# Local attention: the second half of the transposed softmax weights is copied by VectorE, at the head of its step

## The reference, cut to what matters

```
def _L0_attn_ref(x, w_attn, w_proj):
    NUM_HEADS = 16
    WINDOW = 64
    ...
    att = jnp.einsum('bnihd,bnjhd->bnhij', q, k) * scale
    att = jax.nn.softmax(att, axis=-1)
    y = jnp.einsum('bnhij,bnjhd->bnihd', att, v)
    y = y.reshape(B, T, C)
    return jnp.einsum('btc,oc->bto', y, w_proj)
...
    x = x + _layernorm(_L0_attn_ref(_layernorm(x, axis=-1), L0_attn_w_attn, L0_attn_w_proj), axis=-1)
```

## Time and profile before

| | |
|---|---|
| median of 3 runs | 1538.36 us (1538.18 to 1543.03) |
| the profiled execution | 1537.03 us |
| its span, first to last instruction | 1535.2 us |
| mean granted TensorE clock | 0.982 |
| busy over the span: PE, DVE, ACT, POOL | 93%, 55%, 47%, 39% |

### The profile page before, as it was taken

One profiled execution on the slowest core, in us unless ns is written; L12 is line 12 of the kernel. 1 busy time (PEld: TensorE's weight loads), 2 busy tenths in 40 slices (PEclk: granted clock), 3 DMA queues, 4 the chain that ended last, 5 costly groups with the idle time before them and its releaser, 6 DMA issues. The chain is left out here.

```text
span 1535.2 us, 36218 instructions
## 1 busy us (share of the span) xinstructions
PE 1425.0 (93%) x13257; PEld 1244.6 (81%) x13257; DVE 849.5 (55%) x1947; ACT 729.0 (47%) x1688; POOL 605.1 (39%) x1133
## 2 busy tenths in 40 slices
PE   5999999899799999999999997998999999999985
PEld 4777777688799999999999996866777777777865
DVE  3666666456233333333343331365778887888762
ACT  3666666431344444444444542243555555555542
POOL 2555555405122212221222111444566776675442
PEclk9999999999899999999999999999999999999998
DMA  5233333254111111111111112521111112111000
GB/s 194 89 109 112 98 104 94 70 158 138 35 35 43 49 42 42 42 49 42 42 42 42 48 41 64 170 66 47 39 60 46 49 57 62 45 53 43 9 15 22
DMA packets 88045, 100.11 MB, mean 65 GB/s; under 512 B 12384, under 2 KB 74720, under 8 KB 87872
## 3 DMA queue, kind: packets, MB, share of 16 engines
q1 hardware_dynamic: 77824, 75.53, 15.7%
q0 software_dynamic: 6480, 17.70, 4.1%
q10 hardware_dynamic: 3568, 4.55, 0.9%
HBM read 63.28 MB, written 34.47 MB: 64 GB/s over the span
## 5 line engine op out<-in xcount | busy, mean ns | idle before, releaser
L891 PEld LDWEIGHTS ex_hb<-ex_xT,lane_w 128*128 128x128 f32 x3124 | 362.4, 193 | 6.5 <-issue 2.8
L891 PE MATMUL ex_hb<-ex_xT,lane_w 128*128 128x128 f32 x3124 | 363.0, 276 | 2.4 <-ACT lane_w L887 2.4
L994 DVE TENSOR_TENSOR ex_gT<-ex_gT,ex_hb 128x384 f32<-128x384 f32 (+1 forms) x142 | 69.3, 488 | 334.4 <-ACT ex_gT L957 307.1
L865 POOL COPY slot_idx<-source 128x1 int32<-128x1 int32 x69 | 37.6, 544 | 413.0 <-PE ex_xb L918 413.0
L927 PE MATMUL ex_yb<-w,ex_gT 128*128 x852 | 195.7, 379 | 1.6 <-DVE ex_gT L996 1.6
L955 ACT ACTIVATE ex_gT<-ex_hb 128x384 f32<-128x384 f32 (+1 forms) x142 | 62.2, 438 | 246.7 <-PE ex_hb L891 245.9
L927 PEld LDWEIGHTS ex_yb<-w,ex_gT 128*128 128x128 f32 x852 | 156.3, 190 | 20.1 <-issue 1.8
L887 ACT COPY lane_w<-w 128x1408 f32 x71 | 96.9, 1365 | 7.9 <-issue 1.7
L1068 POOL TENSOR_SCALAR la_ln_ve<-la_ln_mv 128x1 f32<-128x1 f32 x128 | 33.4, 261 | 155.6 <-DVE la_ln_mv L1061 150.6
L1639 POOL DMA_INDIRECT la_a<-yg,place x64 | 69.2, 1081 | 49.8 <-POOLq L55 34.6
L1398 DVE TENSOR_TENSOR la_em<-la_E,consts 128x512 f32<-128x512 f32 x128 | 79.3, 681 | 6.6 <-PE la_E L1352 6.5
(11 more groups left out here) (263 smaller groups left out, 3124.7 us busy)
## 6 DMA issues: line engine op xcount, KB each, us to landing
yg<-ex_yo SPq DMA_DIRECT2D x71, 128.0 KB
w<-in_w SPq DMA_DIRECT2D x16, 384.0 KB, 4.8
w<-in_w SPq DMA_DIRECT2D x16, 352.0 KB
w<-in_w SPq DMA_DIRECT2D x16, 320.0 KB
wa_xa<-in_x SPq DMA_DIRECT2D x32, 128.0 KB, 2.1
x<-wa_xo SPq DMA_DIRECT2D x32, 128.0 KB
xn<-wa_xn SPq DMA_DIRECT2D x32, 128.0 KB, 3.5
xn1T<-wa_x1T SPq DMA_DIRECT2D x32, 128.0 KB, 3.5
```

What stands on the lines that cost most here:

```text
L891: o = e.matmul(out, lane_w[:, i % 2, k, at:at + P], B[i % 2]["xT"][:, k, :], start=(k == 0), stop=(k == KC - 1))
L994: o = e.tensor_tensor(g, g, chunks(hb[2 * half + 1][:, 0:n], c1 - c0), ALU.mult)
```

## The change

ScalarE no longer copies the second half. VectorE does it, as the first work of the step behind (step s - 4 = i where ScalarE had it at s - 3 = i), with the same waits ahead of it and the same semaphore after it. ScalarE keeps the first half, at its old place. No other line differs.

```
             for s in range(STEPS):
+                for i in tile(s, 4, NT):
+                    e.wait_ge(S["pTp"], i + 1)
+                    if i >= 2:
+                        e.wait_ge(S["pv"], i - 1)
+                    e.tensor_copy(B[i % 2]["pT"][:, 4:8, :], chunks(bP[:, 1], 4)).then_inc(S["pTb"], 1)
                 for i in tile(s, 3, NT):
                     d = B[i % 2]
                     e.wait_ge(S["S"], i + 1)
...
                     if i >= 2:
                         e.wait_ge(S["pv"], i - 1)
                     e.copy(B[i % 2]["pT"][:, 0:4, :], chunks(bP[:, 0], 4)).then_inc(S["pTa"], 1)
-                    e.copy(B[i % 2]["pT"][:, 4:8, :], chunks(bP[:, 1], 4)).then_inc(S["pTb"], 1)
```

## The result

The changed kernel takes 1524.8 us, the median of 4 runs (1521.97 to 1526.08), beside 1538.27 us for the kernel before (1536.88 to 1543.03, 4 runs). The ratio is 0.9899, with a 95% interval of 0.9877 to 0.9922: it is 1.0% faster. Forecast were 1523.5 us and a range of 1518.5 to 1530. The profiled execution took 1526.08 us, its span is 1524.2 (before: 1535.2), the mean granted clock 0.978 (before: 0.982).

The account below looks back on a forecast made before the run. TensorE was taken to bound the kernel, standing still ahead of L410 for the `pT` copies. 31 steps x 0.48 us = 14.9 us, so 1538.4 - 14.9 = 1523.5 us, range 1518.5 to 1530.

Parts of the forecast that it names:

- The bound and the mechanism: TensorE, busy 93% of the span, bounds; its wait ahead of L410 ends earlier once L743 leaves ScalarE.
- The forecast stall: TensorE's stall ahead of L410: 0.27 us of the 0.76 stay, still released by ScalarE.
- The price of VectorE's copy: VectorE's copy out of PSUM to `pT`: 0.70 us for 512 columns, costing nothing in an idle gap of 1.29 us.
- The gain of a step: Product of L410: 0.49 us earlier, less 0.01, so 0.48 us per step; 8.07 us instead of 8.55.
- the constant 0.10 us: Between the end of ScalarE's releasing copy and the product of L410: 0.10 us, before and after the change.
- The 0.01 us charged: ScalarE's copy L742: 0.01 us longer because both engines read two PSUM banks at the same time.
- Tile 0 gave nothing: First product: gain lost, as TensorE next waits for L1081's normalised tile; its 1.86 us idle time just gets longer.
- the cover of VectorE's copy: TensorE's 1.09 us of scores, which L607 must await anyway, hide VectorE's copy with 0.2 us to spare.
- its allowance: Half-clock stretches falling differently: 1.4 us per group of eight matmuls, three groups allowed, 4 us both ways.
- The longer copy: Rival: VectorE's copy takes 1.23 us, product only 0.37 us earlier per step, 1526.9 us; chance 0.06.
- Another wait taking the place: Rival: another semaphore of L410, or a later wait in the step, swallows the gain, 1538.4 us; chance 0.08.
- The slower case: Rival: VectorE's copy held behind late `wa_xo` statistics; at 1.6 us later each step loses 0.4, 1550.8 us; chance 0.04.

## Why the prediction was right

**The bound and the mechanism held.** TensorE's only wait in the step was the one ahead of L410, and it ended with the second half on ScalarE. Splitting the wait with both copies left on ScalarE gave nearly the same gain (0.51 us a step), and putting ScalarE's load back took none of it.

**ScalarE's half didn't move.** L747 starts 1.66 us after `qT` in both profiles (187.34 - 185.68; 185.06 - 183.40), and TensorE still waits for it. The forecast stall was 0.27 us, measured 0.22.

**The price of VectorE's copy.** Forecast 0.70 us by the line through two plain copies, measured 0.69; the start was forecast 0.08 us after the transposes, measured 0.03. It was covered as said: L612 was not late.

**The gain of a step was mis-sized by 0.06 us.** I took 0.48 us from the ends of the copies, and it was 0.54. The step that failed is the constant 0.10 us between ScalarE's end and the product: it is 0.05 where TensorE's list is stopped at its first wait, `pTa`, and 0.10 at its second, `pTb`, and the change moves it from the second to the first. That is 31 x 0.05 = 1.5 us more than in my sum. The 0.01 us charged for two engines reading PSUM at once was not paid: ScalarE's copy took 592 ns (median of 32), and 591 ns before. In a steady step this says little, as the two copies overlap for 0.12 us only (185.06 to 185.18). For the last tile they start together, and neither is slower than elsewhere:

```profile
278.81 0.58 ACT L747 COPY wa_pT<-wa_P 128x512 f32<-128x512 f32 x1 [7.37 <-PE wa_P L484]
278.81 0.69 DVE L608 COPY wa_pT<-wa_P 128x512 f32<-128x512 f32 x1 [7.79 <-PE wa_P L484]
```

The Trainium skill's rule ("PSUM — Partial Sum Buffer", Specifications), full bandwidth in parallel as long as the banks differ, holds for this pair of copies. What costs ScalarE's copy L743 its 12 ns beside L607 in the kernel before (603 ns in steady steps, 591 for the last tile), no run shows.

**Tile 0 gave nothing, as forecast.** L420 behind the first product starts at 27.69 instead of 28.22, but the pipeline was 0.54 us ahead already before the first copy of the change: the subtraction of tile 0's maxima starts at 19.09 instead of 19.63. TensorE's idle time there grew from 1.86 to 2.40 us, by what the product won. The product of the last tile gained 0.38 us, not 0.48: both copies start together there, VectorE's is the longer one, and the wait is for `pTb` again. The prediction took the cover of VectorE's copy from the scores, and behind the last tile there are none.

**The clock took its allowance and more, and the total was near in part by luck.** The changed kernel was 0.5 us ahead at the start, which the change doesn't explain; 30 steps won 0.54 us each, so 16.2, and the last one 0.4. The profiled execution lost 1.7 us before the last product at half clock (3.20 + 2.31 against 1.89 + 1.89 us in two groups). That makes 15.4 us, and the last product was 15.5 ahead. Behind it another 3.7 + 0.8 us were lost, and the end was 11.0 ahead. So the two groups and the stretches behind them took 5.4 us more than in the profile before, where I had allowed 4 for the clock. By the median the change gave 13.5 us of the 14.9 forecast. The mechanism itself was worth 16.6, and the step that I sized too small offset part of what the clock took.

**A slip in the range.** Its lower end is named as the clock's 4 us and the uncharged hundredth (0.3 us); from 1523.5 that gives 1519.2, not 1518.5. The measured 1524.8 lies inside either way.

**The rivals.** The longer copy is refuted by its row. Another wait taking the place: none did. The slower case needed `wa_xo` 1.2 us late; in the profile after VectorE is free at 184.24, 0.25 us before it starts the copy. That the place in VectorE's list matters as this rival said is shown by moving the copy behind the maxima and the subtraction, 2.5 us of work: 3.25 us of stall.

## What to carry to other kernels

When one wait per step holds the bounding engine, ask what exactly it needs first: half the data may be enough, and the order of the consumer's own work can hide the rest. Splitting the wait gave about as much as moving the copy (0.51 and 0.54 us a step), and both together 0.83. The copy put on VectorE was free because VectorE would have waited there anyway: behind 2.5 us of other work in the list, the same copy cost ten times what it had won.

## What the runs showed that I had not expected

- The place in a list of waits has a price: TensorE starts 0.05 to 0.06 us after the release when it is stopped at the first wait of its list, 0.10 to 0.11 us when at the second, as the steady steps of nine kernels here show (before, changed and seven variants).
- TensorE idle for 3.25 us in every step (18 of them in 229 us, so 12.7 us each on average, and 13.6 us from tile 8 on) was granted 0.82 of full speed on average; to the 94 us of the waits alone came 69 more.
- A wait of 2.10 us was followed by half clock in some executions and by full clock in others of nearly the same program: full clock in the profile before and with both halves on VectorE, half clock in the seven other profiles with a wait of 2.1 to 2.2 us there. In the four profiles where the shared expert's group fills it, full clock followed each time. What decides where the wait stands stays open.
- The same kernel took 1538 us on one chip and 1525 to 1527 on two others, for the most part in a stage that no edit touched; ratios held (0.9899 three times).
